# Attention in a Perceiver kernel: the softmax shift of every pair's last tile added by VectorE, and the context's high part made by GpSimd

## The reference

```
x: (32, 64, 256), ctx: (32, 1601, 256)
x = x + attention(layernorm(x), ctx)       # 16 heads of 16, keys and values from ctx
x = x + ssm(layernorm(x))
x = x + experts(layernorm(x))
attention: Q = xn @ W_Q + b_Q;  K = ctx @ W_K + b_K;  V = ctx @ W_V + b_V
           softmax(Q K^T / 4) V, joined over the heads, @ W_O + b_O
```

## Time and profile before

| | us |
|---|---|
| three timed runs | 2362.01, 2364.93, 2363.89 (median 2363.89) |
| the profiled execution, its own time | 2363.51 |
| its span in the trace | 2361.8 |
| attention, from the first key matmul to the last mix | 40 to 1453 |
| TensorE busy | 2154.9 (91%) |
| VectorE busy | 1444.9 (61%) |
| ScalarE busy | 1239.7 (52%) |
| GpSimd busy | 797.4 (34%) |
| exponentials L570 | 416, mean 1.026 |
| matmuls L660 that add the shift | 832, together 166.5 |
| maxima L507 | 1024, mean 0.570 |
| low part of the context L467 | 128, mean 1.815 |

### The profile page before, as it was taken

How to read it: one execution, slowest core, us unless ns; L and a number is a source line. 1 busy time by engine, 2 the same in 40 slices (tenths; PEclk the granted TensorE clock), 3 DMA queues, 4 the chain that set the end, 5 groups by cost and what they waited for, 6 DMA issues and landing times. The chain is left out here.

```text
span 2361.8 us, 65032 instructions
## 1 busy us (share of the span) xinstructions
PE 2154.9 (91%) x28672; PEld 1768.7 (75%) x28672; DVE 1444.9 (61%) x2610; ACT 1239.7 (52%) x1667; POOL 797.4 (34%) x571
## 2 busy tenths in 40 slices
PE   5999999999999999999999997896799997499993
PEld 3789999999999999999999995643233336499993
DVE  4655556555555555565555552427588875688885
ACT  2355555555555555555555553363799971255661
POOL 2222222222222222222222212012699962255551
PEclk8999999999999999999999998987899998699997
DMA  2111111111111111111111103004875521466663
GB/s 90 36 49 46 40 48 39 47 42 39 47 42 40 51 42 41 48 39 47 41 39 48 43 16 103 4 5 185 216 173 145 143 81 55 158 223 224 223 221 123
DMA packets 130685, 197.40 MB, mean 84 GB/s; under 512 B 17714, under 2 KB 108850, under 8 KB 130243
## 3 DMA queue, kind: packets, MB, share of 16 engines
q1 hardware_dynamic: 120594, 176.58, 24.9%
q0 software_dynamic: 4416, 12.06, 1.5%
q10 hardware_dynamic: 5392, 4.59, 0.6%
HBM read 161.60 MB, written 31.59 MB: 82 GB/s over the span
## 5 line engine op out<-in xcount | busy, mean ns | idle before, releaser
L507 DVE TENSOR_REDUCE max_part<-work 128x1 f32<-128x384 f32 (+1 forms) x1024 | 539.2, 570 | 239.7 <-PE work L635 216.2
L570 ACT ACTIVATE probs<-scores 128x1024 f32<-128x1024 f32 (+1 forms) x416 | 423.8, 1026 | 397.5 <-PE scores L660 381.5
L467 POOL TENSOR_TENSOR ctx_lo<-ctx_whole,ctx_hi 128x768 fp32r<-128x768 f32 (+1 forms) x128 | 232.3, 1815 | 1034.2 <-DVE ctx_hi L490 1034.2
L502 DVE SCALAR_TENSOR_TENSOR keys_lo<-work,bk,keys_hi 128x384 fp32r<-128x384 f32 (+1 forms) x256 | 162.6, 636 | 262.2 <-ACT keys_hi L549 262.2
L1193 POOL TENSOR_TENSOR decay<-steps_in,xn 128x1024 f32<-128x1024 f32 x126 | 243.2, 1965 | 53.4 <-DMA steps_in<-scratch_results 39.7
L625 PE MATMUL work<-wv_hi,ctx_hi 128*128 128x256 f32 (+1 forms) x832 | 243.9, 293 | 2.1
L654 PE MATMUL scores<-q_hi,keys_hi 64*128 64x256 f32 (+1 forms) x1664 | 241.9, 283 | 0.0
L654 PE MATMUL scores<-q_lo,keys_hi 64*128 64x256 f32 (+1 forms) x1664 | 237.2, 277 | 0.0
L654 PE MATMUL scores<-q_hi,keys_lo 64*128 64x256 f32 (+1 forms) x1664 | 237.1, 277 | 0.0
L625 PE MATMUL work<-wv_hi,ctx_lo 128*128 128x256 f32 (+1 forms) x832 | 234.4, 282 | 0.0
L674 PE MATMUL acc<-probs,values 128*17 128x64 f32 x13312 | 230.5, 220 | 4.0 <-ACT probs L570 4.0
(11 more groups left out here) (234 smaller groups left out, 4685.4 us busy)
## 6 DMA issues: line engine op xcount, KB each, us to landing
xs<-in_w_T SPq DMA_DIRECT2D x46, 1024.0 KB
ctx_whole<-in_ctx_T SPq DMA_DIRECT2D x96, 384.0 KB, 3.2
steps_in<-scratch_results SPq DMA_DIRECT2D x256, 128.0 KB, 2.7
ctx_whole<-in_ctx_T SPq DMA_DIRECT2D x32, 449.0 KB, 3.5
scratch_results<-steps SPq DMA_DIRECT2D x16, 512.0 KB, 2.6
scratch_mixed<-mixed ACTq DMA_DIRECT2D x32, 128.0 KB, 1.7
mixed_b<-scratch_mixed SPq DMA_DIRECT2D x4, 1024.0 KB, 13.6
scratch_z<-z SPq DMA_DIRECT2D x16, 256.0 KB, 2.5
```

The lines of the kernel that those rows point to most:

```text
L467: nc.gpsimd.tensor_tensor(ctx_lo[c][:, :, 0:n], s.ctx_whole[c % 2][:, :, 0:n], ctx_hi[c][:, :, 0:n].bitcast(F32), ALU.subtract).then_inc(l ...
L502: nc.vector.scalar_tensor_tensor(keys_lo[par][:, m, start:start + n], bank[:, 0:n], s.bk[:, m:m + 1], keys_hi[par][:, m, start:start + n]. ...
L507: nc.vector.reduce_max(max_part[par][:, place(pair), c:c + 1], bank[:, 0:CHUNKS[c][1]], AX) \
L570: nc.scalar.activation(probs[slot][0:rows, :], scores[slot][0:rows, :], ACT.Exp, scale=1.0 / HD ** 0.5).then_inc(exp_done, 1)
```

## The change

In every pair (and for tile 12 alone) the last tile no longer gets the two L660 matmuls: seven tiles of thirteen, 1, 3, 5, 7, 9, 11 and 12, called `SHIFTED`. In their place VectorE adds a 128 x 1024 tile `wide` to the scores in PSUM, in place, and ScalarE's exponential of that tile waits for this addition and no longer for TensorE. `wide` holds the shift on all 128 rows and is made once a batch: two new units "wide" at the end (two matmuls of 512 columns, ones times `shifts`), each copied to SBUF by ScalarE. TensorE issues them after the mix of tile 12, before the next batch.

VectorE's list follows the tiles now: the units ahead of a tile, then the addition if the tile is one of the seven, then the units behind the pair. From the second batch on, GpSimd makes the context's high part itself, by a multiplication with one, right before it makes the low part.

```diff
+LAST_UNITS = [("wide", 0), ("wide", 1)]
+UNITS = [unit for tiles, before, after in PAIRS_OF_TILES for unit in sum(before, []) + after] + LAST_UNITS
+SHIFTED = [t for tiles, _, _ in PAIRS_OF_TILES for t in tiles[-1:]]
-COPIED_KINDS = ("v",)
+COPIED_KINDS = ("v", "wide")
...
             def split(b, c):                                   # GpSimd
                 n = even(CHUNKS[c][1])
+                if b >= 1:
+                    pool.wait_ge(s.ctx_loaded[c % 2], (b * (NC // 2) + c // 2 + 1) * 16)
+                    pool.wait_ge(unit_done, (b - 1) * NU + LAST_OF_CHUNK[c] + 1)
+                    nc.gpsimd.tensor_tensor(ctx_hi[c][:, :, 0:n], s.ctx_whole[c % 2][:, :, 0:n],
+                                            s.one[:, :].rearrange("p (a b) -> p a b", a=1).to_broadcast([P, KD, n]),
+                                            ALU.mult).then_inc(hi_split, 1)
...
+            def shift(b, par, t):                              # VectorE
+                n = b * NT + t
+                rows = TILES[t][1]
+                bank = scores[(par * NT + t) % 2]
+                dve.wait_ge(scores_ready, n + 1)
+                if t == SHIFTED[0]:
+                    wait_evacuated(dve, b, WIDE[1])
+                nc.vector.tensor_tensor(bank[0:rows, :], bank[0:rows, :], wide[par][0:rows, :], ALU.add) \
+                    .then_inc(shifted, 1)
+            def attend(b, par, ahead):
+                for tiles, before, after in BESIDE:
+                    for t, units in zip(tiles, before):
+                        if ahead:
+                            prepare(b + 1, 1 - par, units)
+                        if t in SHIFTED:
+                            shift(b, par, t)
+                    if ahead:
+                        prepare(b + 1, 1 - par, after)
...
+                elif UNITS[u][0] == "wide":                    # ScalarE
+                    h = UNITS[u][1]
+                    act.wait_ge(unit_done, b * NU + u + 1)
+                    if b >= 2:
+                        act.wait_ge(shifted, (b - 1) * NS)
+                    nc.scalar.copy(wide[par][:, h * BANK:(h + 1) * BANK], bank[:, :]).then_inc(unit_copied, 1)
...
-                        act.wait_ge(scores_ready, n + 1)
+                        if t in SHIFTED:
+                            act.wait_ge(shifted, b * NS + SHIFTED.index(t) + 1)
+                        else:
+                            act.wait_ge(scores_ready, n + 1)
...
+                elif kind == "wide":                           # TensorE
+                    h = UNITS[u][1]
+                    wait_evacuated(pe, b, ROW)
+                    last = nc.tensor.matmul(bank[:, :], ones[side(h), :], shifts[side(h), :], start=True, stop=True)
...
-                if t == 0:
-                    wait_evacuated(pe, b, ROW)
-                for h in range(2):
-                    last = nc.tensor.matmul(bank[0:rows, h * BANK:(h + 1) * BANK], ones[side(h), 0:rows],
-                                            shifts[side(h), :], start=False, stop=True, skip_group_check=True)
+                if t not in SHIFTED:
+                    for h in range(2):
+                        last = nc.tensor.matmul(bank[0:rows, h * BANK:(h + 1) * BANK], ones[side(h), 0:rows],
+                                                shifts[side(h), :], start=False, stop=True, skip_group_check=True)
...
+                if ahead:
+                    for u in WIDE:
+                        unit(b + 1, 1 - par, u)
```

More of the change, by code:

```diff
@@ L353 @@
 ]
-UNITS = [unit for tiles, before, after in PAIRS_OF_TILES for unit in sum(before, []) + after]
+LAST_UNITS = [("wide", 0), ("wide", 1)]
+UNITS = [unit for tiles, before, after in PAIRS_OF_TILES for unit in sum(before, []) + after] + LAST_UNITS
+SHIFTED = [t for tiles, _, _ in PAIRS_OF_TILES for t in tiles[-1:]]
+NS = len(SHIFTED)
 NU = len(UNITS)
 ROW = UNITS.index(("row",))
+WIDE = [UNITS.index(unit) for unit in LAST_UNITS]
 LAST_MAX = max(u for u in range(NU) if UNITS[u][0] == "max")
@@ L397, in attention @@
         shifts = sb("shifts", [P, BANK], F32R)
+        wide = [sb(f"wide{i}", [P, HEADS * LATENTS]) for i in range(2)]
         ones = sb("ones_row", [P, P], F32R)
@@ L415, in attention @@
         shift_made = sem("shift_made")
+        shifted = sem("scores_shifted")
         exp_done = sem("exp_done")
@@ L484, in _, with split_first @@
         def _(dve):
-            def split(b, c):
+            def split_first(c):
                 n = even(CHUNKS[c][1])
[L487 to L491, removed]
+                dve.wait_ge(s.ctx_loaded[c % 2], (c // 2 + 1) * 16)
+                nc.vector.tensor_copy(ctx_hi[c][:, :, 0:n], s.ctx_whole[c % 2][:, :, 0:n]).then_inc(hi_split, 1)
             def unit(b, par, u):
@@ L521, in unit, with prepare @@
                         .then_inc(unit_evacuated, 1)
-            def prepare(b, par, more=True):
-                for u in range(NU):
+            def shift(b, par, t):
[7 more added lines that the diff above has]
+                    .then_inc(shifted, 1)
+            def prepare(b, par, units):
+                for u in units:
                     if UNITS[u][0] not in COPIED_KINDS:
                         unit(b, par, u)
-                    if more and u in LAST_OF_CHUNK:
-                        split(b + 1, LAST_OF_CHUNK.index(u))
+            def attend(b, par, ahead):
[7 more added lines that the diff above has]
+                        prepare(b + 1, 1 - par, after)
             nc.vector.memset(acc[:, :], 0.0)
@@ L535, in _ @@
             for c in range(NC):
[L536 to L539, removed]
+                split_first(c)
+            prepare(0, 0, range(NU))
+            for b in range(batches):
+                attend(b, b % 2, b + 1 < batches)
         @block.scalar
```

3 lines of the change are left out of this document (2 added, 1 removed).

## The result

| | before | after |
|---|---|---|
| timed runs, us | 2362.01 to 2364.93, median 2363.55 (4) | 2459.96 to 2463.0, median 2461.67 (4) |
| ratio after / before | | 1.0415, 95% interval 1.0397 to 1.0433 |
| span of the profiled execution | 2361.8 | 2460.4 |
| the period: one batch in steady state (from one row matmul to the next, 700 to 1050 us) | 43.18 | 45.94 |
| last batch, from the mix of the batch before it to its own last mix | 25.9 | 37.4 |

The change costs 4.15%, 98 us. The forecast was 2452 with a range of 2422 to 2485.

What follows compares the result with a forecast made beforehand. TensorE, balanced against VectorE's maxima to about 0.1 us, was taken to bound attention. Per batch -0.235 + 1.48 + 1.38 = +2.63 us, times 31 is +81; last batch +7, first wide units +0.3: +88, 2452 us, range 2422 to 2485.

Steps and rivals of the forecast that it cites:

- the pairs' waits: Five pairs with maxima, (2, 3) to (10, 11): delays of 2 x 0.48 + 0.30 + 0.12 + 0.10 = 1.48 us a batch.
- the last batch: Last batch: the second exponential waits for the addition, about +0.95 us for each of six pairs and tile 12: +7.
- The first step: Attention: TensorE and VectorE are balanced to about 0.1 us; in five pairs the saved 0.23 us turns into waiting.
- k1 waits for max5: Pairs (2, 3), (4, 5), (6, 7): max5 stands behind the addition, so k1 starts +0.48, +0.48 and +0.30 us later.
- Tile 12: Batch's end: the mix starts +1.04 us later behind its exponential, the next batch's first scores +1.38 us.
- The addition: VectorE's 128 x 1024 addition in PSUM: 1.22 us for its result and 1.18 for the queue.
- GpSimd: Last chunk's high part adds at most about 2.16 us on GpSimd: cost 0, with 1.2 us of cover.
- The rival with the clock: TensorE's clock falls at every batch's end, about 5 us a batch at half speed: +78, 2530 us; chance 3%.
- The bounds: Shorter addition -10 us, longer one +33, tile 12's 1.04 hidden -32; likeliest case 2425 to 2485 us.
- the saving comes through: Rival: VectorE's addition is covered everywhere, 44 us go, less the last batch's loss of 7: 2327 us; chance 4%.
- Only the batch's end costs: Rival: slack covers the pairs' waits but not tile 12's, 1.15 us a batch: 2407 us; chance 6%.
- GpSimd comes late: Rival: GpSimd's high part takes over 3.3 us or holds up VectorE; at 4.3 us, 2483 us; chance 4%.

Runs made afterwards that it cites:

- experiment 5: Kernel after the change, with the addition on only 512 of the 1024 columns: 2381.29 us, ratio 1.0057.
- experiment 9: Kernel before the change, with max3 issued ahead of the first tile's L660 (its halves swapped) and max4 behind it: 2354.52 against 2365.42 us, ratio 0.9951.
- experiment 3: Kernel after the change, with tiles 3, 5 and 7 given back to TensorE's matmuls: 2408.33 us, ratio 1.0189.
- experiment 4: Kernel after the change, with tile 12 alone given back to TensorE's matmuls: 2447.69 us, ratio 1.0344.
- experiment 10: Kernel after the change, with only tile 1 shifted by addition and the wide units kept: 2384.08 us, ratio 1.0079.
- experiment 8: Kernel after the change, with VectorE and not GpSimd making the context's high part: 2465.44 us, ratio 1.0413.
- experiment 1: Kernel before the change, with only the context's high part moved to GpSimd from the second batch on: 2366.66 against 2364.95 us, ratio 1.0010.
- experiment 6: Kernel after the change, with max5 and max6 ahead of the addition on VectorE's list: 2490.87 us, ratio 1.0518.
- experiment 7: Kernel after the change, with no additions in the last batch, which takes its shifts by matmul: 2451.73 us, ratio 1.0353.
- experiment 2: Kernel before the change, with max3 and max4 both issued ahead of the first tile's L660: 2384.16 us, ratio 1.0084.

## Why the prediction was right

The forecast held: 2452 against 2461.67, 10 us or a tenth of the change too low, by the mechanisms it named. Two terms were too small, the pairs' waits and above all the last batch, and two steps came out right with the help of something that their working did not have.

- *The first step, that TensorE at 99.87 of 100 is balanced against VectorE and not ahead of it*, stands. In experiment 5 each of the five pairs with maxima has lost a matmul pair and lasts as long as before to 0.01 us. In experiment 9 nothing is removed, only max3 comes to VectorE sooner, and they get shorter.
- *k1 waits for max5.* Shown by the trace after, and by experiments 3 (without these three additions their pairs are as before, -1.45 a batch of the 1.46 worked out from the trace) and 5 (with half the addition the wait is gone). The hold itself came as worked out: k1 stands 1.60 behind k0, 1.64 forecast. The terms were nevertheless 0.03 to 0.08 too small, because a unit that starts after a wait also starts slower. From k1's first row to its next are 0.44 to 0.46 us (as for k0, 696.09 - 695.63 = 0.46), where a row in the stream takes 0.35 (696.44 - 696.09). The rows show k1's weight load starting with its matmul, at 697.23, and so not hidden behind a running one; that this is where the 0.10 comes from is my reading of them. Before, k1 was in the stream; now it pays these 0.10. With it the pairs add up: (2, 3) 0.44 + 0.10 = 0.54 (0.55 measured); (6, 7) 1.60 - 1.34 + 0.11 = 0.37 (0.38); (8, 9), where v to v is 1.59, 1.59 - 1.52 + 0.11 = 0.18 (0.19). The sum of the five was 1.48; it is 1.80, 0.32 more. Pair (0, 1) and the batch's end, 0.11 and 0.08 less than forecast, take 0.2 of that back, which leaves a batch 0.12 longer than forecast (2.75 against 2.63).
- *Tile 12.* The addition begins at 729.18, 0.09 before `neg_max` ends (729.08 + 0.19), an overlap that the working had for the maxima and left out here. The mix waits 1.12 us for its exponential and stands 0.96 later in its part of the batch (4.12 in place of 3.16), forecast 1.04. The end's sum, 1.38, was 1.30 for that reason. But its parts were put together wrongly. "The `shifts` for it are made at 736.0, in time" is true only because the mix is late: take the late mix away and the wide pair waits for them (experiments 4 and 10, 0.68 us a batch). Two delays lie one above the other here, and undoing the larger gives back 0.50 only.
- *The addition* took 1.224 us, taken as 1.22 from the scan's row.
- *GpSimd* costs nothing in the kernel after (its trace, and experiment 8). Its last mask ended at 737.73 and the first maximum came at 738.89, a cover of 1.16 us; 1.2 was forecast. That this agrees is luck in part: a high part of 2.16, less the cast that it waited for (0.63 for this size), ends the mask at 743.2 and not at 742.7, and leaves 0.7. The high part took 1.69. And the cover is that of the late batch's end: experiment 1, without it, has GpSimd in front of the first maximum, 0.10 a batch.
- *The last batch* is the term that was mis-sized: 7 forecast, 11.5 measured. At full clock a pair there took 4.87 us in place of 3.83, which is 1.04 where 0.95 a place was taken, and makes the 7. Then the clock fell to 0.57, and from mix to mix the next three pairs took 6.39, 6.32 and 5.97. The rival with the clock was looked for at every batch's end, where it stayed at 1.00; it came true in one batch, the one that I had charged at full speed. Its longest gaps ahead of the fall are 1.33 us, little more than the 1.12 of the batches' ends, but they come one after another.
- *The bounds.* Six places at +0.16 in 31 batches are +30, not the +33 that the working gives, and its lower end of 2425 is neither 2452 - 10 nor 2452 - 32. The result lies far enough inside that neither matters.

The rivals: *the saving comes through* falls with the result and with experiment 10, in which the one saving that does come through is 0.23 us a batch. But the number put up against it, that an addition would have to take 0.5 us to be free, was too strict: experiment 5's 0.69 was free. By the rows themselves it may take some 0.78 (from 702.10 to k1's 703.39, less 0.55 for max5 and 0.04 behind it, plus the 0.08 of overlap). *Only the batch's end costs* falls with experiment 3: three pairs carry 1.45 of 2.75. *GpSimd comes late* falls with the trace after, in which the mask is 1.16 us early; in the kernel before it would have been true by 0.10 (experiment 1).

Open: the 1.5 us ahead of the first row and behind attention, the 2.5 us of experiment 10 behind attention, and why pair (0, 1) gained 0.34 in after but 0.23 in experiment 10. The last goes with tile 12: the pair takes 6.47 or 6.48 wherever tile 12 has its addition (after, experiments 3, 5 to 8) and 6.58 or 6.59 where it has not (4 and 10). There the wide pair waits 0.30 for `shifts`, and k0 follows the last scores row by 0.30 rather than 0.21.

## What to carry to other kernels

Before work is moved off an engine that looks fully busy, find what its instructions wait for within 0.1 us of starting; here it was the reductions of the very engine that received the work, so in the five pairs with maxima the saving was nothing and the cost whole. An operation put on an engine with 40% idle time costs what stands behind it on that engine's list: ask for each place who needs the next item, and when; the same addition was free at 0.69 us and cost 0.5 at 1.22. Where two engines hand banks to each other, reordering the issue so that the waited-for chain starts earlier (experiment 9) can win where moving work loses. The Trainium skill, "Perfetto Trace Analysis", section "Optimization Strategy", says to find the gaps on the engine that is to be improved, and what blocks it there. The trace agrees, with the qualification that here the gap of 0.28 at 702.23 shows only in a row of the weight loads while the engine counts as 99.87 busy.

## What the runs showed of the hardware that I had not expected

- The granted clock fell in the last batch from 1.00 to 0.57 (of 2.4 GHz, so for most of that stretch the lower level of 1.2) after repeated waits of 0.4 to 1.33 us and none longer; TensorE was busy 5.30 of 8.00 and 1.60 of 3.00 us ahead of the fall. In experiment 7, busy 7.89 and 8.88 of 10.00 there, it stayed at 1.00. At the batches' ends single waits of 1.12 us left it at 1.00. It also fell in the last batches of experiments 3, 4, 6 and 8 (0.80, 0.66, 0.66 and 0.66 over the 5 us in which it first fell) and not in that of experiment 5, whose waits between 1450 and 1472 were 0.41 to 0.80, nor in that of experiment 10. I had looked for one long gap; here many short ones stood ahead of the fall. The Trainium skill, "TensorE: Matmul & The Clock Gate", section "What's actually happening", puts the clock down to how busy the engine has recently been, with which this agrees.
- A matmul that starts after a wait cost some 0.10 us beyond the wait here (0.44 to 0.46 to the next row in place of 0.35).
- The two halves of the partitions run side by side as two streams, and a wait that hits only one shifts it by 0.18 us until the next matmul that takes the whole array, which waits for the later one (experiment 2: +0.13 a pair). The order in which the halves alternate was worth half a matmul pair of 512 columns (0.13 of 0.235).
- GpSimd's 1.5 us of additional reading and writing, 124 times, did not slow VectorE: its maxima took a mean of 568 ns, and 570 before; `keys_lo` of 384 columns 617 and 619. The Trainium skill, "SBUF — State Buffer", section "SBUF: two separate sides", restricts the contention of these two engines to VectorE's 2-port modes and to operations with two SBUF inputs. Neither of these two operations is one, as both read PSUM, and the trace agrees.
